# Node spans, duplicates and degrees of a four-layer graph kernel regrouped

## The reference

```python
# layer 0: relational mean        msg = (h @ weight_r[etype])[src] / deg[dst];  M = segment_sum(msg, dst)
#          x += where(deg > 0, relu(0.2 h + 0.8 M), h)
# layer 1: attention              e = tanh([h[src], h[dst]] @ W_attn.T + b) @ w_out
#          alpha = segment_softmax(e, dst);  x += segment_sum(alpha * h[src], dst)
# layer 2: Chebyshev, K = 3       dis = 1 / sqrt(segment_sum(edge_weight, src)), 0 where that is 0
#          w = -dis[src] * edge_weight * dis[dst];  two propagations segment_sum(w * t[src], dst)
#          x += (1 - sigmoid(...)) * tanh(...)
# layer 3: GCN                    x += segment_sum(edge_weight * (h @ W)[src], dst) + bias
```

## Time and profile before

| | us |
|---|---|
| median of 3 timed runs | 2012.38 |
| lowest, highest | 2007.74, 2017.11 |
| span of the profiled execution | 2533.2 |

### The profile page before, as it was taken

The page is one execution under the profiler, slowest core; times in us unless marked ns, Lnnn a source line. Parts: engine busy times, 40 slices in busy tenths (PEclk is TensorE's granted clock), DMA queues, the critical chain, the costliest instruction groups (busy, mean ns, idle before and its releaser), DMA issues.

```text
span 2533.2 us, 28723 instructions
## 1 busy us (share of the span) xinstructions
PE 1374.4 (54%) x7844; PEld 1089.7 (43%) x7845; DVE 991.2 (39%) x2889; ACT 200.8 (8%) x390; POOL 1235.7 (49%) x1381
## 2 busy tenths in 40 slices
PE   4455555565621556566555651111111898879877
PEld 2455554554511456556555640000000898434423
DVE  7555554554604333334333440000000676300488
ACT  2000000000000111111111100000000111000200
POOL 1666666666672366565666677677777000000000
PEclk8766767677755555555555555555555898899989
DMA  5444343435200222222222200000000002988878
GB/s 165 150 155 153 120 152 118 150 121 168 65 1 0 68 63 66 65 62 64 66 66 64 66 21 0 0 0 1 0 0 0 0 0 103 353 335 353 326 295 336
DMA packets 154645, 272.07 MB, mean 107 GB/s; under 512 B 44030, under 2 KB 100154, under 8 KB 151546
## 3 DMA queue, kind: packets, MB, share of 16 engines
q1 hardware_dynamic: 111322, 229.57, 24.9%
q0 software_dynamic: 40064, 41.32, 6.6%
q10 hardware_dynamic: 3232, 0.82, 0.1%
HBM read 215.32 MB, written 56.29 MB: 107 GB/s over the span
## 4 chain that ended last, share of the span: by engine, by line
another core or an unknown queue 28%; PE 26%; issue 20%; DVE 14%; POOL 5%; DMA 4%; DVEq 1%; ACT 1%; SPq 1%; POOLq 0%; ACTq 0%
PE acc L987 10%; PE acc L1035 7%; POOL rings L736 5%; PE acc L1029 4%; DVE rings L1367 2%; DVE big L1826 2%; DMA big<-pairs_by_src 2%; DVE rings L1401 2%; DVE rings L1402 1%; DVE big L1391 1%; DMA rings<-local_rows 1%; PE acc L1009 1%; DMA relation_rows<-big 1%; DMA rings<-relation_rows,idx_ring 1%
## 5 line engine op out<-in xcount | busy, mean ns | idle before, releaser
L987 PE MATMUL acc<-rings 128*65 128x128 f32 x3328 | 576.1, 326 | 634.4 <-issue 459.6
L987 PEld LDWEIGHTS acc<-rings 128*65 128x65 f32 x3328 | 456.0, 168 | 709.4 <-issue 694.3
L736 POOL DMA_INDIRECT rings<-relation_rows,idx_ring x416 | 409.5, 984 | 281.9 <-issue 184.1
L736 POOL DMA_INDIRECT rings<-attention_rows,idx_ring x416 | 394.6, 948 | 305.1 <-issue 234.3
L1029 PE MATMUL acc<-attend_mem,rings 128*128 x1664 | 373.8, 411 | 266.2 <-issue 182.3
L1029 PEld LDWEIGHTS acc<-attend_mem,rings 128*128 128x128 f32 x1664 | 367.3, 328 | 273.0 <-issue 273.0
L753 POOL DMA_INDIRECT pairs_by_src<-fed_val,fed_idx x416 | 405.6, 975 | 149.4 <-issue 120.0
L1425 DVE TENSOR_SCALAR rings<-iota_bf,col_local,score 128x256 f32<-128x256 bf16 x416 | 139.4, 408 | 480.3 <-remote 371.8
L786 POOL DMA_INDIRECT big<-support_rows,ext_node x4 | 3.9, 963 | 450.6 <-DMA support_rows<-big 449.7
L1680 DVE TENSOR_TENSOR rings<-acc,rings 128x512 f32<-128x512 f32 x52 | 35.6, 684 | 352.0 <-remote 343.9
L1035 PE MATMUL acc<-big,attend_mem 128*64 128x512 f32 x700 | 163.0, 600 | 9.1 <-DMA big<-pairs_by_src 9.1
(11 more groups left out here) (279 smaller groups left out, 895.0 us busy)
## 6 DMA issues: line engine op xcount, KB each, us to landing
big<-pairs_by_src SPq DMA_DIRECT2D x54, 2048.0 KB, 12.5
pairs_by_src<-zeros SPq DMA_DIRECT2D x24, 1792.0 KB
big<-key_rows SPq DMA_DIRECT2D x52, 512.0 KB
rings<-local_rows SPq DMA_DIRECT2D x52, 256.0 KB
big<-pairs_by_src SPq DMA_DIRECT2D x12, 1024.0 KB, 12.3
rings<-relation_rows,idx_ring POOLq DMA_INDIRECT x416
pairs_by_src<-fed_val,fed_idx POOLq DMA_INDIRECT x416
rings<-attention_rows,idx_ring POOLq DMA_INDIRECT x416
```

The source lines that it names most:

```text
L736: pool.indirect_dma_start(ring[h][:, u, 0:width], None, table, bass.IndirectOffsetOnAxis(ap=idx_ring[h][:, u:u + 1], axis=0),).then_inc(ga ...
L987: m = pe.matmul(node_sums[:, bass.ds(at[u] * P + w * P, P)], rows[h][:, u, :], onehot[h][:, u, w * P:(w + 1) * P], start=False, stop=False ...
```

## The change

- A tile's nodes are now sought in one span of 128 nodes that starts at its first destination (`window_first`, at most `TOP`), so that `onehot` is 128 wide and `add_up` issues one matmul to a tile. To let a span cross a block's border, the sums lie in eight PSUM banks, each starting 384 nodes after the one before and so overlapping it by 128 (`SPAN`, `sum_at`); `turn_nodes` adds the two parts of a block that lies in two banks. The eight banks leave none for other sums in this loop.
- Duplicates: `key_rows` also holds the edge weights. DVE compares keys, multiplies by weights and sums (`dup_val`), one operation each to a half of eight tiles. The eight matmuls L998, `take_dups`, `indices` and the dump area go; every edge of a cell now writes the cell's sum to it.
- Degrees: `onehot_lo`, `onehot_hi`, `hi_parts` and the degree matmuls move from the relation loop to the attention loop (`degree_hots`, on DVE behind `onehot_rows` and ahead of the addition; on PE behind the look-up). `dis` and its kin are computed behind the one-hots of the aggregation.
- One-hots are made for eight tiles by one operation (`window_hots`, a tensor_tensor with both inputs broadcast), the transposed ones by two operations instead of eight.
- In the aggregation the softmax weight goes into the rows (ACT, one scaled copy to a tile, `weigh_rows`) instead of the one-hots.

```diff
+    SPAN = BANK - P
+    TOP = VB * P
+    SUM_BANKS = 8
+    assert SUM_BANKS * SPAN == TOP and SPAN % P == 0 and NODES == TOP + P
+    PER_SPAN = SPAN // P
...
-            def copy_rows():
+            def weigh_rows():
 
                 with act.Fori(0, IT) as it:
                     for h in range(2):
                         act.wait_ge(slot_free["agg"], it * 2 + h + 1)
-                        act.activation(rows[h][:, :, :], edge_rows[:, bass.ds(it * (2 * H) + h * H, H), :], ACT.Copy
-                                       ).then_inc(rows_copied, 1)
+                        for u in range(H):
+                            t = bass.ds(it * (2 * H) + (h * H + u), 1)
+                            o = act.activation(rows[h][:, u, :], edge_rows[:, t, :].rearrange("p a c -> p (a c)"), ACT.Copy,
+                                               scale=weight_e[:, t])
+                        o.then_inc(rows_weighted, 1)
...
                     for h in range(2):
                         _, at = nc.values_load_multi_w_load_instructions(
-                            block_at[0:1, bass.ds(it * (2 * H) + h * H, H)], engines=[PE_ENGINE], min_val=0, max_val=NB - 1,
-                            skip_runtime_bounds_check_because="a node's block, below NB")
+                            sum_at[0:1, bass.ds(it * (2 * H) + h * H, H)], engines=[PE_ENGINE], min_val=0,
+                            max_val=SUM_BANKS * BANK - P, skip_runtime_bounds_check_because="a window's column, within a bank")
                         pe.wait_ge(onehot_ready[key], it * 2 + h + 1)
                         if key == "rel":
                             pe.wait_ge(gathered[key][h], (it + 1) * (16 * H))
                         else:
-                            pe.wait_ge(rows_copied, it * 2 + h + 1)
+                            pe.wait_ge(rows_weighted, it * 2 + h + 1)
                         for u in range(H):
-                            for w in range(2):
-                                m = pe.matmul(node_sums[:, bass.ds(at[u] * P + w * P, P)], rows[h][:, u, :],
-                                              onehot[h][:, u, w * P:(w + 1) * P],
-                                              start=False, stop=False, skip_group_check=True)
-                            if key == "rel":
-                                if u % (H // 2) == H // 2 - 1:
-                                    m.then_inc(rows_free[key], 1)
-                                m = pe.matmul(degree_bank[:, degree_at:degree_at + 3 * NB], onehot_lo[h][:, u, :],
-                                              hi_parts[h][:, u, :], start=False, stop=False, skip_group_check=True)
-                        if key == "rel":
-                            pe.wait_ge(dups_read, it * 2 + h + 2)
-                            for u in range(H):
-                                m = pe.matmul(dup_bank[:, u * 7:(u + 1) * 7], eq[h][:, u, :],
-                                              dup_right[:, bass.ds(it * (2 * H) + (h * H + u), 1), :]
-                                              .rearrange("p a c -> p (a c)"), start=True, stop=True, skip_group_check=True)
-                        m.then_inc(slot_free[key], 1)
+                            m = pe.matmul(node_sums[:, bass.ds(at[u], P)], rows[h][:, u, :], onehot[h][:, u, :],
+                                          start=False, stop=False, skip_group_check=True)
+                            if key == "rel" and u % (H // 2) == H // 2 - 1:
+                                m.then_inc(rows_free[key], 1)
+                        if key == "agg":
+                            m.then_inc(slot_free[key], 1)
 
             def turn_nodes(k):
 
-                pe.wait_ge(sums_by_act, (k + 1) * (MAIN // 2 + 1))
-                pe.wait_ge(sums_by_dve, (k + 1) * (MAIN // 2))
+                pe.wait_ge(sums_by_act, (k + 1) * (SUM_BANKS // 2))
+                pe.wait_ge(sums_by_dve, (k + 1) * (SUM_BANKS // 2))
                 for b in range(NB):
                     c = b // PER_BANK * BANK + b % PER_BANK * D1
-                    t = pe.matmul(acc[:, c:c + D1], sums_t[0:D1, b * P:(b + 1) * P], ident[0:D1, 0:D1],
-                                  start=True, stop=True, skip_group_check=True)
+                    i = sum_bank(b)
+                    x = i * BANK + b * P - i * SPAN
+                    twice = 0 < b == i * PER_SPAN
+                    t = pe.matmul(acc[:, c:c + D1], node_sums_t[0:D1, x:x + P], ident[0:D1, 0:D1],
+                                  start=True, stop=not twice, skip_group_check=True)
+                    if twice:
+                        t = pe.matmul(acc[:, c:c + D1], node_sums_t[0:D1, x - P:x], ident[0:D1, 0:D1],
+                                      start=False, stop=True, skip_group_check=True)
...
+                        pe.wait_ge(degree_hots_ready, it * 2 + h + 1)
+                        for u in range(H):
+                            m = pe.matmul(degree_bank[:, 0:3 * NB], onehot_lo[h][:, u, :], hi_parts[h][:, u, :],
+                                          start=False, stop=False, skip_group_check=True)
+                        m.then_inc(degrees_added, 1)
...
                 for w in range(2):
-                    for e in range(0, H * P, 2 * P):
-                        o = dve.tensor_scalar(onehot_t[h][:, w, e:e + 2 * P], local_ring[h][:, e:e + 2 * P],
-                                              iota_part[:, w:w + 1], None, ALU.is_equal)
+                    o = dve.tensor_scalar(onehot_t[h][:, w, :], local_ring[h][:, :], iota_part[:, w:w + 1], None, ALU.is_equal)
                 o.then_inc(onehot_ready[key], 1)
 
...
+            def window_hots(h, cols):
+
+                return dve.tensor_tensor(onehot[h], iota_bf[:, 0:P].unsqueeze(1).to_broadcast([P, H, P]),
+                                         col_window[:, cols].unsqueeze(2).to_broadcast([P, H, P]), ALU.is_equal)
+
+            def degree_hots(it, h):
+
                 cols = bass.ds(it * (2 * H) + h * H, H)
...
+                dve.wait_ge(degrees_added, it * 2 + h + 1)
+                dve.tensor_tensor(onehot_hi[h], iota_bank.unsqueeze(1).to_broadcast([P, H, NB]),
+                                  col_hi[:, cols].unsqueeze(2).to_broadcast([P, H, NB]),
+                                  ALU.is_equal).then_inc(hi_ready, 1)
+                dve.tensor_tensor(onehot_lo[h], iota_bf[:, 0:P].unsqueeze(1).to_broadcast([P, H, P]),
+                                  col_lo[:, cols].unsqueeze(2).to_broadcast([P, H, P]), ALU.is_equal)
+                dve.wait_ge(hi_ready, it * 2 + h + 2)
+                for k in range(3):
+                    o = dve.tensor_tensor(hi_parts[h][:, :, k * NB:(k + 1) * NB], onehot_hi[h],
+                                          degree_parts[:, cols, k:k + 1].to_broadcast([P, H, NB]), ALU.mult)
+                o.then_inc(degree_hots_ready, 1)
 
             def relation_hots():
 
                 dve.sem_inc(rows_free["rel"], 4)
                 dve.sem_inc(keys_read, 2)
-                dve.wait_ge(table_stored["rel"], 16 * 5)
-                dve.tensor_copy(iota_bank, iota_row[:, 0:NB]).then_inc(hi_ready, 1)
-                dve.wait_ge(hi_ready, 1)
-                with dve.Fori(0, IT - 1) as it:
-                    relation_step(it)
-                dve.wait_ge(dups_read, 2 * (IT - 1))
-                indices(col_key, idx_by_src, slice(0, EARLY))
-                relation_step(IT - 1)
-
-            def weighted_hots():
+                with dve.Fori(0, IT) as it:
+                    for h in range(2):
+                        cols = bass.ds(it * (2 * H) + h * H, H)
+                        dve.wait_ge(keys_here[h], (it + 1) * 16)
+                        dve.tensor_tensor(eq[h], key_ring[h][:, :, 0:P], col_key[:, cols].unsqueeze(2).to_broadcast([P, H, P]),
+                                          ALU.is_equal).then_inc(eq_ready, 1)
+                        dve.wait_ge(rows_free["rel"], it * 4 + 2 * h + 2)
+                        window_hots(h, cols).then_inc(onehot_ready["rel"], 1)
+                        dve.wait_ge(eq_ready, it * 2 + h + 1)
+                        dve.tensor_tensor(eq[h], eq[h], key_ring[h][:, :, P:2 * P], ALU.mult).then_inc(keys_read, 1)
+                        dve.wait_ge(keys_read, it * 2 + h + 3)
+                        dve.tensor_reduce(dup_val[:, cols], eq[h], AX.X, ALU.add).then_inc(dups_ready, 1)
+
+            def sum_hots():
 
                 with dve.Fori(0, IT) as it:
                     for h in range(2):
                         dve.wait_ge(slot_free["agg"], it * 2 + h + 1)
-                        for u in range(H):
-                            col = bass.ds(it * (2 * H) + (h * H + u), 1)
-                            o = dve.tensor_scalar(onehot[h][:, u, :], iota_bf[:, :], col_local[:, col], weight_e[:, col],
-                                                  ALU.is_equal, ALU.mult)
-                        o.then_inc(onehot_ready["agg"], 1)
```

(10 more changed lines are left out.)

## The result

The kernel after takes 2091.3 us (median of 4 runs, 2082.86 to 2093.91), the kernel before 2012.08 (2007.74 to 2017.11). The ratio is 1.038, interval 1.0359 to 1.040: slower by 79 us, where 1981 was forecast and 2050 was the end of the range.

A forecast was written before the change was run, and what follows sets the result against it. POOL's descriptor work was taken as the bound up to the late scatter's end; 2012 + 1 (preparation) + 1 (POOL beside DVE) - 33 (waits) = 1981 us, with an 8 in 10 range of 1905 to 2050.

The forecast's parts named there:

- POOL is the bound: All stages up to the late scatter's end: POOL's descriptor work for indirect DMAs sets the time in the timed run.
- PE, DVE, key rows, degrees, aggregation, preparation at 0 or 1 us: Work beside POOL in the loops and aggregation: hidden, 0 us each; preparation, ended before the relation table landed, +1.
- The crawl: PE's slow matmul starts, every 1.4 to 2.8 us beside scatters: taken as belonging mostly to the profiled execution.
- My POOL sum: Start, gathers and scatters on POOL alone 1652 us, plus 296 behind it: 1948 without a crawl.
- rival A: PE's crawl also in the timed run; if aggregation took 386 of its 417 us there, all 60 go: 1935; chance 0.16.
- my 2290 for the profile after: Whole profiled execution: 2533 us falls to about 2290 as the crawl shrinks with PE's records.
- The 60 us of waits: Median less POOL's sum, about 60 us: shared as relation 26, hole 11, attention 18, scatters 5.
- the -33: Waits: relation falls to 4, hole to 2, scatters to 3, attention stays; 33 us gained.
- rival C: POOL held up by DVE's long two-input operations, 0.25 us for a us: 64 us more, 2044; chance 0.22.
- B: Nothing on POOL's path changes; the 60 us are fixed time or landings: 2014, within 2002 to 2022; chance 0.20.
- POOL beside DVE, +1: Indirect DMAs beside DVE: 315 us of new two-input operations at 0.05 cost 16, 15 go; ends -15 and +64.

The follow-up runs named there:

- e5: Kernel after, with weights in the key rows broadcast in the first step alone, later steps bringing only keys (512 KB instead of 1 MB): 2090.57 us for 2091.3.
- e6: Kernel after, with the 123 padding edges spread over 64 source nodes instead of one; on the chip of the 2538 us: 2415.04 us, ratio 0.9507.
- b1b: Kernel before, with two 1024 wide transposed one-hots in the attention loop in place of eight of 256; on a usual chip: 2029.66 us, ratio 1.0082.

## Why the prediction was wrong

**POOL is the bound: right.** It fills every stage up to its last scatter; in the usual traces it doesn't even wait in the hole between early scatter and attention (0.3 us). **PE, DVE, key rows, degrees, aggregation, preparation at 0 or 1 us: right.** The attention gathers' idle time is unchanged (132.3 and 132.0) with the degrees in their loop; L987 ends at 1409 us, 363 before POOL; POOL starts its gathers at 58.9 us for 59.4; e5 shows the broadcast. The four dense passes are as before: behind the landing 292 us before (2008.4 - 1716.6) and 291 after (2081.0 - 1789.8).

**The crawl: wrong.** I took it for the profiled execution's. It showed on one chip, timed runs included; whether it is the chip or a state that the chip was in isn't shown. My POOL sum from that trace was still near (1948 for 2008), because its durations for POOL are nearly free of it. But on such a chip rival A's mechanism is the one that counts, and a kernel with the change (e6) is 5% faster. Its span, 2405.5, stands against my 2290 for the profile after, so I overrated the gain there: 2533 - 2290 = 243 us for 2533 - 2406 = 127 (e6 has the padding apart too). Rival A's 386 of 417 us I can't get back from the rows; nothing hangs on it.

**The 60 us of waits and the -33: the first failed step.** I took the difference between a sum and a median for waits and shared it out as the disturbed trace shares its own. None of it was waits. This -33 stood in the forecast and in rival C alike, and B, the one case without any gain in the waits, had no price for POOL beside DVE; so the range ended at 2050.

**POOL beside DVE, +1: the second failed step, and the larger.** The term measured +65 (excess 41 to 106): the 16 us that I gave to the new operations were 86, and the 15 that go were 20. I took the tensor_tensor of the earlier trace rows that cost nothing; that was luck of place, since this scatter had started 0.07 us ahead of it, and a gather or scatter already under way isn't held by a two-input operation. What I should have asked is what happens to one that starts inside: the 1.57 us scatter in the same rows was that case. A gather that starts with r us of the operation left ends at r + 0.82 us, so it loses r - 0.13 of its 0.947. For a stream of DMAs with a period of 1.25 us, an operation of length D that meets them at random would then cost about (D - 0.13) squared / 2.5 us, an estimate from these lengths: 0.02 us at the 0.353 us of the earlier trace rows, 0.48 at 1.22. Measured, it was 0.26 on average at 1.22 us (67 us for 260 operations). Four operations of 256 columns merged into one of 1024 didn't cost the same, they cost twice as much (33 and 67 us). Second, I priced only the two-input operations; the transposed one-hots alone cost 16.6 us in b1b.

**Rival C had the mechanism**, named the 0.25 us for a us and a rise of 64 for 65 measured. That the two agree so well is partly luck: its rate came from one scatter beside two scans, the two-input operations cost 67 us rather than its 79, and the 19 us of the transposed one-hots, which it didn't have, made up for it. Without the -33, and with the landing, it would have read 2012 + 1 + 64 + 11.6 = 2089 for 2091.3.

**The landing, +11.6: not in the sum at all.** I told that every edge of a cell now writes to it, and priced the matmuls that went, but not the writes. They stand on the path at the one place where it counts, behind the last scatter. With the three steps put right the sum reads 1981 + 33 + 64 + 11.6 = 2090, for 2091.3.

## What to carry to other kernels

Where GpSimd issues indirect DMAs back to back and is the bound, the instructions of an engine with time to spare aren't free: look for DMAs longer than their median beside VectorE operations with two SBUF inputs, or wide `tensor_scalar` ones, and judge a merge of such operations by the length of what POOL may have to sit out, not by the instructions saved alone. A gap between a sum and a median is not waits until a trace shows a wait. And before a profile's long stretch is laid to the profiler, run the same kernel once more, on another chip if there is one.

## What the runs showed of the hardware that I had not expected

- An indirect DMA that POOL starts inside a VectorE operation with two SBUF inputs ends 0.82 us after that operation does (a scatter 0.84), up to 1.04 us late for 1.22 us operations; a gather that had started before takes its 0.947 us. A reduction of the same length leaves it alone.
- A 1024 wide `tensor_scalar` of 0.75 us with one SBUF input holds a gather at its start in the same way, and one under way until 0.12 us after its end.
- Eleven 128 wide operations in a row held one gather for 3.15 us.
- A scatter of 128 elements in which 123 write one DRAM cell lands in 18 us; with at most two writes to a cell, in 2.2 to 2.9.
- The same kernel takes 2011 to 2013 us on two chips and 2538 on another, where PE takes a record only every 1.9 us on average while POOL issues the late scatters (237 in 459 us). What makes that chip different wasn't found.
